# A third gate scratch buffer, and the gate one projection later, in an eight-core ABC-attention and expert-mixture block

## What is computed

```python
g = (hidden_states @ Wg).reshape(b, t, H, DV)          # H=16, DV=128
o = o * rsqrt(mean(o*o, axis=-1, keepdims=True) + EPS) * g_norm_weight
o = o * (g * sigmoid(g))
attn = o.reshape(b, t, H*DV) @ Wo
x = layernorm(x + attn)
h = relu(x @ W1 + b1);  alpha = softmax(h @ W2 + b2)
ffn = sum_k alpha_k * (U_k (V_k x))
x = layernorm(x + ffn)
```

## Time and profile before

| what | us |
|---|---|
| runs shown, lowest / median / highest (2 runs) | 1921.09 / 1943.7 / 1966.32 |
| profiled execution, its own time | 1932.68 |
| its span (first to last instruction, slowest core, core 2) | 1930.9 |
| spans of the eight cores | 1892.3 to 1930.9 |
| PE busy in the span | 1340.2 (69%) |
| DVE, ACT, POOL busy | 532.7 (28%), 408.7 (21%), 229.4 (12%) |
| the four gate passes on core 2, first projection to last `ofm` copy | 782 to 829, 829 to 873, 1547 to 1594, 1593 to 1637 |

### The profile page before, as it was taken

How to read it: one execution, slowest core, us unless ns; L and a number is a source line. 1 busy time by engine, 2 the same in 40 slices (tenths; PEclk the granted TensorE clock), 3 DMA queues, 4 the chain that set the end, 5 groups by cost and what they waited for, 6 DMA issues and landing times.

```text
span 1930.9 us, 18642 instructions; the slowest of 8 cores (1892.3 to 1930.9 us)
## 1 busy us (share of the span) xinstructions
PE 1340.2 (69%) x6704; PEld 655.7 (34%) x6800; DVE 532.7 (28%) x886; ACT 408.7 (21%) x552; POOL 229.4 (12%) x220
## 2 busy tenths in 40 slices
PE   3458889968985554778685758977555478859563
PEld 1124444434443333333232323423333333324231
DVE  2013332241002222343421272000222244351135
ACT  0000000001124444321200131112444432120013
POOL 2100000000001111341100001101111144010000
PEclk9669999989995555788677868988555588767786
DMA  9940100014214000558945149962300055992502
GB/s 179 180 83 22 45 23 22 22 44 97 35 13 76 1 1 1 88 88 181 204 74 87 30 82 232 166 101 35 53 1 1 1 87 88 207 165 43 87 1 87
DMA packets 61514, 146.24 MB, mean 76 GB/s; under 512 B 7536, under 2 KB 12016, under 8 KB 56048
## 3 DMA queue, kind: packets, MB, share of 16 engines
q0 software_dynamic: 54800, 102.90, 34.6%
q1 hardware_dynamic: 5472, 33.76, 5.2%
q10 hardware_dynamic: 1152, 8.39, 1.1%
HBM read 237.45 MB, written 8.39 MB: 127 GB/s over the span
## 4 chain that ended last, share of the span: by engine, by line
PE 50%; DVE 15%; DMA 15%; ACT 8%; issue 6%; POOL 4%; DVEq 1%; ACTq 0%; POOLq 0%
PE fb L245 48%; DMA wvb<-wv 6%; DMA wob<-wo 4%; DMA w1b<-w 3%; PE tb L245 2%; POOL wbf L265 2%; ACT rbuf L265 1%; DMA wsb<-ws 1%; DVE x1bufs L265 1%; DMA wkb<-wk 1%; DVE msq L265 1%; DVE st L265 1%; DVE xmf L265 1%; DVE sm L265 1%; ACT wrw L265 1%
## 5 line engine op out<-in xcount | busy, mean ns | idle before, releaser
L245 PE MATMUL fb<-w1b,x2fm 128*128 128x512 bf16 x496 | 138.3, 443 | 38.2 <-DMA w1b<-w 36.8
L245 PE MATMUL fb<-wob,ofm 128*128 128x512 bf16 x500 | 136.5, 443 | 10.7 <-DMA wob<-wo 9.4
L245 PE MATMUL fb<-wvb,xpf 128*128 128x512 bf16 x503 | 119.0, 395 | 31.2 <-DMA wvb<-wv 30.7
L245 PE MATMUL fb<-wgb,xmf 128*128 128x512 bf16 x500 | 126.3, 415 | 4.5 <-DVE psf L265 3.6
L245 PE MATMUL fb<-wvb,xmf 128*128 128x512 bf16 x501 | 115.4, 390 | 13.5 <-DMA wvb<-wv 13.0
L265 DVE TENSOR_TENSOR okb<-fb,rbuf 128x256 f32<-128x256 f32 x32 | 13.6, 425 | 304.8 <-ACT rbuf L265 168.7
L245 PEld LDWEIGHTS fb<-w1b,x2fm 128*128 128x128 bf16 x512 | 55.0, 110 | 114.8 <-issue 92.2
L245 PE MATMUL fb<-wsb,xpf 128*128 128x512 bf16 x249 | 69.8, 443 | 32.9 <-DMA wsb<-ws 17.7
L245 PEld LDWEIGHTS fb<-wob,ofm 128*128 128x128 bf16 x512 | 56.4, 111 | 90.3 <-issue 84.4
L245 PEld LDWEIGHTS fb<-wvb,xpf 128*128 128x128 bf16 x512 | 50.7, 100 | 96.7 <-issue 42.3
L265 DVE TENSOR_TENSOR s1f<-s1f,fb 64x256 f32<-64x256 f32 (+1 forms) x48 | 24.1, 501 | 208.6 <-PE fb L245 206.9
(11 more groups left out here) (149 smaller groups left out, 1890.7 us busy)
## 6 DMA issues: line engine op xcount, KB each, us to landing
strip<-x_main SPq DMA_DIRECT2D x24, 1024.0 KB, 9.6
wvb<-wv POOLq DMA_DIRECT2D x16, 1024.0 KB, 34.0
wgb<-wg POOLq DMA_DIRECT2D x16, 1024.0 KB, 20.2
wob<-wo POOLq DMA_DIRECT2D x16, 1024.0 KB, 21.8
w1b<-w POOLq DMA_DIRECT2D x16, 1024.0 KB, 21.3
strip<-x_pre SPq DMA_DIRECT2D x8, 1024.0 KB, 8.2
wqb<-wq POOLq DMA_DIRECT2D x8, 1024.0 KB, 29.2
y<-x1bufs ACTq DMA_DIRECT2D x8, 1024.0 KB, 4.6
```

Source lines behind the costliest of these rows:

```text
L245: t.matmul(o, l, r, start=a, stop=b, is_transpose=(True if tpp else None)))
```

## The change

A third `gsc` buffer of 4 KB per partition is added, the index of the buffer is taken modulo 3 in place of 2, and `g_gate` is called two chunks behind `g_proj` and not one. Everything that a call issues stays the same, in number and form. The order of PE becomes P0, P1, P2, T0, P3, T1, T2, T3, and that of DVE E0, E1, D0, copies of T0, E2, D1, copies of T1, E3, D2, copies of T2, D3, copies of T3. One more buffer is freed at the end of the gate.

```diff
-            gsc2 = [AR.alloc("gsc", [128, GV], F32) for _ in range(2)]
-            gsc2_free = [None, None]
+            gsc2 = [AR.alloc("gsc", [128, GV], F32) for _ in range(3)]
+            gsc2_free = [None, None, None]
...
-                            gsc2[c % 2].ap(0, 128, g * 512, cn),
+                            gsc2[c % 3].ap(0, 128, g * 512, cn),
                             bk[g][0:128, 0:cn]),
-                            waits=[mG_of[c], gsc2_free[c % 2]]
-                            + gsc2[c % 2].birth)
+                            waits=[mG_of[c], gsc2_free[c % 3]]
+                            + gsc2[c % 3].birth)
...
-                    gsc = gsc2[c % 2]
+                    gsc = gsc2[c % 3]
...
-                    gsc2_free[c % 2] = sg
+                    gsc2_free[c % 3] = sg
...
-                for c in range(NHC + 1):
+                for c in range(NHC + 2):
                     if c < NHC:
                         g_proj(c)
-                    if c - 1 >= 0:
-                        otb_free = g_gate(c - 1, vh)
+                    if c - 2 >= 0:
+                        otb_free = g_gate(c - 2, vh)
                     if c < NHC:
                         g_evac(c)
...
-            for b in (msq, otb, obs, sgs, gsc2[0], gsc2[1]):
+            for b in (msq, otb, obs, sgs, gsc2[0], gsc2[1], gsc2[2]):
```

## The result

The changed kernel took 1900.23 us in the median against 1920.99 for the kernel before; these medians are over all executions. In some executions of either kernel the cores of one half of the chip, sometimes of both, run at a lower clock and take some per cent longer, and the ratios and intervals in this document leave those out. The ratio is 0.9904, with a 95% interval of 0.9888 to 0.9921: 18.4 us less, inside 2% and clear of the spread. Forecast were 6.0 us less, from 1932.7.

A forecast was written before the change was run, and what follows sets the result against it. PE idled 42.2 us before the `otb` transposes, in the fill and drain of the gate's passes. Fill gains less drain costs gave 8.4 us, less 2.4 for the clock, 6.0: from 1932.7 to 1926.7 us, range 1908 to 1948.

The forecast's parts named there:

- The wait of P2 for its banks: In first gate passes, P2 waits until E0 empties its banks; a gap of 2.6 to 2.8 us.
- the waits that T0 and T1 lose: In the gate passes, T0 and T1 start without waits; before, T0 waited 6.97 us in the first pass.
- the drain: End of each gate pass, T1's start to T3: 10.56 us, 4.64 more than before, as `obs` and `sgs` are single.
- the Wo load that moves along: Load of Wo's second half, 39.38 and 40.69 us, issued when the gate is over, moves with the gate's end.
- The sum at full pace: Gate's four passes, fill gains less drain costs: 7.03 + 6.61 + 6.86 + 6.47 - 4 x 4.64 = 8.4 us gained.
- the second rival: Gate: P2 starts slow in all four passes, losing 4 x 2.1 = 8.4 us, the whole gain; 1932.7 us, chance 0.10.
- the first projection of a second pass ... I leave it as it is: Start of second gate passes, behind a wait before and after: no change counted, 0.8 us allowed either way.
- The clock term: First gate passes: P2 starts at a lower PE clock behind its new gap, 1.2 us lost twice, 2.4 us.
- six projections of the first 400 us: Early projections behind gaps of 1.96 to 2.12 us, mean 8.07 us, taken as the price of P2's gap: 1.2 us.
- that gives 1926.7: Whole kernel: the profiled execution's 1932.7 us less a gain of 6.0 us.
- The range's lower end: Whole kernel: 1908 us, the lowest execution shown less the largest gain and a little.
- The third rival: Gate: P2 and P3 of each pass slow to Wo's 0.311 us per matmul, 23 us lost; 1947 us, chance 0.08.

The follow-up runs named there:

- the repeated comparisons: The changed kernel three times more, beside fresh runs of the kernel before: ratios 0.9966, 0.9954 and 0.9958, medians 1903.5, 1901.4 and 1901.3 us.
- the first comparison: The changed kernel against the kernel before, first time: 1900.23 us against 1920.99, ratio 0.9904.
- Both: The changed kernel with two `obs` and `sgs` and a third pair of PSUM banks; against the kernel before 0.9900 and, again, 0.9897 (1908.0 and 1891.0 us).

## Why the prediction was right and wrong

**The order was right.** The wait of P2 for its banks, the waits that T0 and T1 lose, the drain, the waits left in sum (36 and 5 us forecast, 36.3 and 5.5 measured) and the Wo load that moves along came as the steps had them. "The sum at full pace" gave 8.4 us; the traces give 9.6 for the gate, the repeated comparisons 6.5 to 8.8 for the kernel. By the pieces: first passes 4.6 forecast and 6.0 measured, second passes 3.8 and 3.2.

**Where the gain sits, only the second rival said.** The forecast of the waits, 42.2 against 36 and 5, leaves 1 us. The rest of the 8.4 is nearly all P2, which in before takes 8.9 us in a first pass and 9.4 in a second for what takes 7.07 at full pace: 1.9 and 2.3 us, twice each. The second rival has this in its price, 4 x 2.1; in the sum the clock stands only as a correction of 2.4 at the end. And "the first projection of a second pass ... I leave it as it is" set a term at nothing: with first passes alone changed, the second pass gained 1.0 us.

**The clock term was wrong.** I charged 2.4 us for P2 starting slow behind its new gap, by six projections of the first 400 us. P2 did not start slow: on the cores of the first two traces of the changed kernel, all 32 first-pass P2, behind gaps of 1.2 to 2.9 us, took 7.07 us for 32 matmuls, full pace. The measured price is nothing, the lower bound that the prediction had named. The gaps of rows 6 were no longer, but their projections came behind 32 small matmuls and a first short gap, 4.4 to 4.9 us behind the last full matmul, and the new P2 stands directly behind 64 full ones. So the length of the gap alone was the wrong thing to compare by. Nor does the work ahead settle it alone: P2 of second passes in before comes behind 64 full matmuls too, then T0's wait of 3.1 to 4.7 us and its eight small ones, and in the three traces with that order 41 of 48 ran slow and 7 at full pace, these behind waits of 3.3 to 3.4 us. Which of the differences matters was not tried.

**The base was wrong, and that put the time out of the range.** The step "that gives 1926.7" started from the profiled execution's 1932.7, set by core 2, with core 3 next. I named the spans of the cores as the first view and took nothing from them but the core; six of eight lay at 1892 to 1901. What set these two behind goes with the granted clock of 0.81, which the result section shows on them alone. The range's lower end stood on the lower of two runs, 1921.1, from the same occasion. With 1910 us, which before took in every later comparison, the same sum gives 1904 with the clock term and 1901.6 without it; measured were 1900 to 1904.

**The third rival rested on the wrong reading of Wo.** The 0.311 us per matmul and the granted clock of 0.73 were those of core 2. On core 0 of the same execution the stretch of rows 8 reads (same columns):

```profile
873.00:1001.00 128.00, 97.76 (x460) 44.96 (x458) 50.33 (x76) 20.43 (x16) 13.25 (x18) 0.85 0.90 173
```

The clock is that of the gate, 0.85, and Wo's second half took 0.241 us per matmul on core 0 and 0.289 on core 2, from its first to its last. So most of the slow pace was no property of that stage, and nothing of the kind came to P2 and P3. The Trainium skill (TensorE: Matmul & The Clock Gate, Part 1, Seeing it yourself) says that the limiter takes the whole die, four cores of the eight; here two cores of a die had 0.81 while core 0 and core 1 of the same die had 1.00, so on this point the trace does not agree. That cores lose about a fifth of their clock in dense matmuls agrees with it, for these two cores.

**What stays open.** Why before lost about 10 us more in the first comparison than in the others. In its profiled execution that is the clock of two cores from Wo on; for its other executions of that comparison there is neither a trace nor a span by core. Whether the change keeps cores from it, or whether it was a matter of the occasion, was not settled: in the executions that the ratios count the changed kernel never showed it, but in the three later comparisons before didn't either, but for a single one of 1925.5 us. The likelier reading of 0.9904 is that about 8 of the 18 us are the change and the rest is not shown to be.

## What to carry to other kernels

When a pipeline already runs at the pace of its main engine in the middle, one stage more of distance helps the fill and costs in the drain: look which buffer is single (here `obs` and `sgs`), since that chain comes into the open at the end. A wait of the main engine costs more than its length where slow work follows it: count both, here the second was nearly all that was won. Before a sum is made against a profiled execution, compare the cores: where the slowest stands 20 us above the median at a lower clock, base and stage readings taken from it carry a disturbance, and another core's row tells it at once. The price of a gap for PE's clock could not be taken here from a gap of like length elsewhere, where PE had done other work ahead of it.

## What the runs showed of the hardware

In these traces a DVE product and a POOL product that both read SBUF did not run side by side at their own pace. In the kernel with two `obs` and `sgs` the groups by form are:

```profile
L265 POOL TENSOR_TENSOR obs<-obs,gnw 128x1024 f32<-128x1024 f32 x16 | 44.2, 2765 | 2.6 <-POOL obs L265 0.4
L265 DVE TENSOR_TENSOR otb<-obs,sgs 128x1024 bf16<-128x1024 f32 x16 | 28.4, 1772 | 6.8 <-POOL obs L265 5.6
```

In before and in the changed kernel, where the single buffers kept the two apart, they took 2348 and 1225 ns in the mean, and 2349 and 1226 after. The Trainium skill (SBUF — State Buffer, Who interferes with whom) says that a DVE instruction with two SBUF inputs contends with a GpSimd instruction that reads SBUF, and that the order of issue decides which one is blocked. The rows agree: in the lines under "Both" D0 of 2.95 us began 0.03 us behind a POOL product of 1.90 us, and 2.95 is about the rest of that product (1.87) and its own 1.23; POOL's next product, begun 0.94 us before D0's end, took 3.15 us in place of 2.35. The copies out of PSUM beside POOL's products kept their 1.49 us a pair, in every kernel. So part of what the second buffers could gain was lost again: 9.9 us came of the 12 forecast, and D2's 0.46 us in each of the four passes is 1.8 of the 2.1 missing.
